# A two-layer graph network on one core: index buffers doubled from two to four, with the loops of GpSimd and SyncE unrolled over two bodies

## The reference, cut to what matters

```python
h   = node_features @ W_l1 * node_attr          # per node: 64 scalars and 32 vectors of 3
w   = silu(edge_scalars @ W_fc1) @ W_fc2        # per edge: 192 or 224 weights
hs  = h[edge_src]                               # gather, 160 floats for each edge
msg = products of w, hs and edge_attr           # per edge
agg = segment_sum(msg, edge_dst)                # scatter to the destination node
out = layernorm(x + self_term + agg @ W_out ...)
```

## Time and profile before

| | us |
|---|---|
| median of 3 runs | 7637.68 (7616.32 to 7642.06) |
| the profiled execution, its own time | 7651.23 |
| its span, first to last instruction | 7649.5 |
| PE matmul busy | 4892.6 (64%) |
| PE weight load busy | 3438.5 (45%) |
| POOL busy | 3010.1 (39%) |
| ACT busy | 2927.0 (38%) |
| DVE busy | 2467.3 (32%) |
| mean granted TensorE clock | 0.732 |

### The profile page before, as it was taken

How to read it: one execution, slowest core, us unless ns; L and a number is a source line. 1 busy time by engine, 2 the same in 40 slices (tenths; PEclk the granted TensorE clock), 3 DMA queues, 4 the chain that set the end, 5 groups by cost and what they waited for, 6 DMA issues and landing times. The chain is left out here.

```text
span 7649.5 us, 230407 instructions
## 1 busy us (share of the span) xinstructions
PE 4892.6 (64%) x91130; PEld 3438.5 (45%) x91131; DVE 2467.3 (32%) x6461; ACT 2927.0 (38%) x12105; POOL 3010.1 (39%) x3206
## 2 busy tenths in 40 slices
PE   6666666666666666666756666666666666666666
PEld 4444444444444444444644444444444444444445
DVE  3322222222222222222433333333333333333335
ACT  3333333333333333333434443444434444444445
POOL 4443434334334443344343333333333333343432
PEclk7777777777777777777877777777767777677777
DMA  3111111111111111111222221222211111111112
GB/s 96 45 45 43 45 44 45 44 43 47 40 38 39 39 39 39 38 39 39 79 55 55 56 57 54 56 55 54 56 53 51 50 49 49 49 51 50 51 49 75
DMA packets 361247, 381.97 MB, mean 50 GB/s; under 512 B 173041, under 2 KB 282421, under 8 KB 361086
## 3 DMA queue, kind: packets, MB, share of 16 engines
q0 software_dynamic: 150528, 257.10, 12.6%
q1 hardware_dynamic: 209360, 122.12, 6.0%
q10 hardware_dynamic: 1296, 1.91, 0.1%
HBM read 357.08 MB, written 23.76 MB: 50 GB/s over the span
## 5 line engine op out<-in xcount | busy, mean ns | idle before, releaser
L531 POOL DMA_INDIRECT e_rows<-scratch_table,k_index x3136 | 2963.1, 945 | 4476.9 <-DMA k_index<-in_src 2819.1
L590 PE MATMUL e_sum<-e_match,e_msg 128*32 128x40 f32 (+1 forms) x81536 | 2567.2, 236 | 2646.0 <-issue 2630.9
L590 PEld LDWEIGHTS e_sum<-e_match,e_msg 128*32 128x32 f32 x81536 | 1874.6, 125 | 3487.1 <-issue 3469.4
L554 ACT ACTIVATE e_match<-e_match,e_attr 128x40 f32<-128x40 f32 x10976 | 2482.7, 315 | 149.1 <-DMA e_attr<-in_edge_attr 118.9
L547 ACT ACTIVATE e_hidden<-e_h 100x512 f32<-100x512 f32 (+1 forms) x784 | 382.8, 488 | 4474.1 <-PE e_h L570 3772.4
L719 DVE TENSOR_TENSOR sums<-sums,e_sum 128x160 f32 x784 | 250.3, 319 | 3586.5 <-PE e_sum L590 1902.3
L583 PE MATMUL e_w<-k_fc,e_hidden 100*128 100x192 f32 (+1 forms) x6272 | 1286.5, 433 | 6.6 <-issue 5.3
L583 PEld LDWEIGHTS e_w<-k_fc,e_hidden 100*128 100x128 f32 (+1 forms) x6272 | 1026.0, 233 | 527.9 <-issue 495.4
L570 PE MATMUL e_h<-e_inputs,k_fc 128*100 128x512 f32 (+1 forms) x1568 | 948.7, 696 | 70.3 <-issue 34.6
L783 DVE TENSOR_TENSOR e_msg<-e_w,e_rows 128x512 f32<-128x512 f32 x784 | 542.2, 692 | 1370.8 <-PE e_w L583 909.7
L788 DVE TENSOR_TENSOR e_msg<-e_w,e_rows 128x384 f32<-128x384 f32 x784 | 429.7, 548 | 0.0
(11 more groups left out here) (130 smaller groups left out, 1059.6 us busy)
## 6 DMA issues: line engine op xcount, KB each, us to landing
e_rows<-scratch_table,k_index POOLq DMA_INDIRECT x3136
e_inputs<-in_inputs SPq DMA_DIRECT2D x196, 256.0 KB
e_attr<-in_edge_attr SPq DMA_DIRECT2D x392, 24.0 KB
e_inputs<-in_inputs SPq DMA_DIRECT2D x196, 40.0 KB
e_xb<-in_xT SPq DMA_DIRECT2D x50, 128.0 KB
scratch_yT<-m_yT SPq DMA_DIRECT2D x10, 640.0 KB, 4.3
e_xb<-scratch_yT SPq DMA_DIRECT2D x50, 128.0 KB
k_index<-in_src SPq DMA_DIRECT2D x392, 4.0 KB, 5.7
```

Source lines behind the costliest of these rows:

```text
L531: pool.indirect_dma_start(out=rows[j][:, t, :], out_offset=None, in_=table_dram, in_offset=bass.IndirectOffsetOnAxis(ap=index[q][:, c:c + ...
L554: last = nc.scalar.activation(match[j][:, t, c, :], match[j][:, t, 4, :], ACT.Copy, scale=attr[q][:, e0 + t, e:e + 1])
L590: return nc.tensor.matmul(out[32 * g:32 * g + 32, c0:c0 + n, :], m[:, f:f + 32], m5[:, which:which + n, :], start=first and opens, stop=en ...
```

## The change

There are four index buffers in place of two. Buffer k belongs to a half body of an even (k = 0, 1) or an odd body (k = 2, 3). In the place where SP loaded the indices of half body 2i+q, it now loads those of half body 2i+q+2, one whole body later, into the buffer whose gathers have just landed. The waits before that load are the same. POOL waits on the semaphore of its own buffer; each buffer is filled once in two bodies, by a semaphore step of 32. To name the buffers in the code, the loops of POOL and SP now cover two bodies in each turn. The other engines' code is unchanged. The setup phase and the node phase load four buffers in place of two, and `src` is padded by two half bodies.

```diff
-    w["index"] = [... (f"k_index{q}", [P, 2 * TPG], I32) for q in range(2)]
+    w["index"] = [... (f"k_index{k}", [P, STEP], I32) for k in range(INDEX_BUFFERS)]
...
-            for q in range(2):
-                sp.dma_start(w["index"][q][:, :], d["src"][:, 2 * TPG * q:2 * TPG * (q + 1)]).then_inc(index_in, 16)
+            for k in range(INDEX_BUFFERS):
+                sp.dma_start(w["index"][k][:, :], d["src"][:, STEP * k:STEP * (k + 1)]).then_inc(index_in, 16)
...
         @block.sync
         def _(sp):
-            def load(i, q):
-                tiles = bass.ds((2 * i + q) * (2 * TPG), 2 * TPG)
-                if not isinstance(i, int):
+            def load(i, q, k):
+                later = not (isinstance(i, int) and i == 0)
+                if later:
                     for j in (2 * q, 2 * q + 1):
                         sp.wait_ge(gathered[j], GATHERED * i)
-                    sp.dma_start(index[q][:, :], d["src"][:, tiles]).then_inc(index_in[q], 16)
+                    sp.dma_start(index[k][:, :], d["src"][:, bass.ds((2 * i + q + 2) * STEP, STEP)]).then_inc(index_in[k], 32)
                     sp.wait_ge(hid_done, GPB * i - GPB + 2 * q + 2)
...
+            def body(i, parity, with_base):
+                for q in range(2):
+                    load(i, q, (2 * parity + q + 2) % INDEX_BUFFERS)
+                if with_base:
+                    load_base(i)
+                if with_base and L == 1 and not (isinstance(i, int) and i == 0):
+                    store_self(i - 1)
+            for parity in range(2):
+                body(parity, parity, True)
+            with sp.Fori(1, NT // 2) as pair:
+                for parity in range(2):
+                    body(2 * pair + parity, parity, True)
             if L == 1:
                 store_self(NT - 1)
-            with sp.Fori(NT, BODIES) as i:
-                load(i, 0)
-                load(i, 1)
+            with sp.Fori(NT // 2, BODIES // 2) as pair:
+                for parity in range(2):
+                    body(2 * pair + parity, parity, False)
+            for k in range(2):
+                sp.wait_ge(index_in[k], 16 * BODIES)
...
         @block.gpsimd
         def _(pool):
-            def gather(count, j):
-                q = j // 2
+            def gather(count, used, parity, j):
+                k = 2 * parity + j // 2
                 if not isinstance(count, int):
                     pool.wait_ge(prepared, 1)
-                    pool.wait_ge(index_in[q], count)
-                    pool.wait_ge(msg_done[j], count)
+                    pool.wait_ge(index_in[k], count)
+                    pool.wait_ge(msg_done[j], used)
+                elif parity:
+                    pool.wait_ge(msg_done[j], 16)
                 for t in range(TPG):
...
-            for j in range(GPB):
-                gather(0, j)
-            with pool.Fori(16, 16 * BODIES, 16) as count:
+            for parity in range(2):
                 for j in range(GPB):
-                    gather(count, j)
+                    gather(0, 0, parity, j)
+            with pool.Fori(32, 16 * BODIES, 32) as count:
+                odd = count + 16
+                pool.compute_val(odd)
+                for parity in range(2):
+                    for j in range(GPB):
+                        gather(count, odd if parity else count, parity, j)
```

More of the change, by code:

```diff
@@ L49 @@
 AHEAD = 2
+STEP = 2 * TPG
+INDEX_BUFFERS = 4
+assert BODIES % 2 == 0 and NT % 2 == 0 and INDEX_BUFFERS == 4
 GATHERED = 16 * TPG
@@ L83, in kept_tensors @@
         w[name] = ctx.enter_context(nc.sbuf_tensor("k_" + name, shape, dt))
-    w["index"] = [ctx.enter_context(nc.sbuf_tensor(f"k_index{q}", [P, 2 * TPG], I32)) for q in range(2)]
+    w["index"] = [ctx.enter_context(nc.sbuf_tensor(f"k_index{k}", [P, STEP], I32)) for k in range(INDEX_BUFFERS)]
     return w
@@ L207, in _ @@
             sp.wait_ge(tab_in, 16)
-            sp.wait_ge(index_in, 32)
+            sp.wait_ge(index_in, 16 * INDEX_BUFFERS)
         @block.gpsimd
@@ L459, in edge_phase @@
         prepared, zeroed = sem("prepared"), sem("zeroed")
-        index_in = [sem(f"index_in{q}") for q in range(2)]
+        index_in = [sem(f"index_in{k}") for k in range(INDEX_BUFFERS)]
         attr_in = [sem(f"attr_in{q}") for q in range(2)]
@@ L475, in _ @@
         def _(sp):
-            def load(i, q):
-                tiles = bass.ds((2 * i + q) * (2 * TPG), 2 * TPG)
-                if not isinstance(i, int):
+            def load(i, q, k):
+                later = not (isinstance(i, int) and i == 0)
+                if later:
                     for j in (2 * q, 2 * q + 1):
                         sp.wait_ge(gathered[j], GATHERED * i)
-                    sp.dma_start(index[q][:, :], d["src"][:, tiles]).then_inc(index_in[q], 16)
+                    sp.dma_start(index[k][:, :], d["src"][:, bass.ds((2 * i + q + 2) * STEP, STEP)]).then_inc(index_in[k], 32)
                     sp.wait_ge(hid_done, GPB * i - GPB + 2 * q + 2)
                 cols = 2 * layer.group_cols
-                if L == 0 and isinstance(i, int):
+                if L == 0 and not later:
                     sp.wait_ge(zeroed, 2)
                 sp.dma_start(inputs[q][0:layer.kin, :], d[f"inputs{L}"][:, bass.ds((2 * i + q) * cols, cols)]).then_inc(inputs_in[q], 16)
-                if not isinstance(i, int):
+                if later:
                     sp.wait_ge(sum_done, GPB * i - GPB + 2 * q + 2)
-                sp.dma_start(attr[q][:, :, :], d["edge_attr"][:, tiles, :]).then_inc(attr_in[q], 16)
+                sp.dma_start(attr[q][:, :, :], d["edge_attr"][:, bass.ds((2 * i + q) * STEP, STEP), :]).then_inc(attr_in[q], 16)
             def load_base(i):
-                if not isinstance(i, int):
+                if not (isinstance(i, int) and i == 0):
                     sp.wait_ge(sum_done, GPB * i - GPB + 2)
@@ L532, in gather @@
                         out=rows[j][:, t, :], out_offset=None, in_=table_dram,
-                        in_offset=bass.IndirectOffsetOnAxis(ap=index[q][:, c:c + 1], axis=0),
+                        in_offset=bass.IndirectOffsetOnAxis(ap=index[k][:, c:c + 1], axis=0),
                     ).then_inc(gathered[j], 16)
-            for j in range(GPB):
-                gather(0, j)
-            with pool.Fori(16, 16 * BODIES, 16) as count:
+            for parity in range(2):
                 for j in range(GPB):
-                    gather(count, j)
+                    gather(0, 0, parity, j)
[5 more added lines that the diff above has]
+                        gather(count, odd if parity else count, parity, j)
         @block.scalar
@@ L1136 @@
     ("attr", (P, NT, 3), F32),
-    ("src", (P, T), I32), ("dst_tile", (P, T), I32), ("dst_by_group", (GP, GQ, GE), I32),
+    ("src", (P, T + 2 * STEP), I32), ("dst_tile", (P, T), I32), ("dst_by_group", (GP, GQ, GE), I32),
     ("edge_attr", (P, T, 6), F32), ("inputs0", (NB0, EPAD), F32), ("inputs1", (2 * NB1, EPAD // 2), F32),
@@ L1198, in lay_out @@
     r["attr"] = by_partition(padded(np.concatenate([a["node_vec1"], a["node_vec1_n2"], a["node_vec1_n3"]], 1), NPAD))
-    r["src"] = by_partition(padded(a["src"], EPAD))
+    r["src"] = by_partition(padded(a["src"], EPAD + 2 * STEP * P))
     dst = padded(a["dst"], EPAD, NODES)
```

8 lines of the change are left out of this document (removed).

## The result

The changed kernel takes **7732.79 us** (median of 4 runs, 7729.44 to 7739.46) against 7638.03 us before: the ratio is 1.0131, with a 95% interval of 1.0111 to 1.0151. It is slower by 95 us, past the upper end of the predicted range, where a small gain was forecast. One of the nine executions of the kernel before that were timed beside e11 and e12 took 14962 us, where the other eight took about 7628; it is left out of their ratios.

The account below looks back on a forecast made before the run. It took PE to be the bound, its sums nearly stopped while POOL gathers. Layer 0's -29 us and layer 1's about 0 summed to -30 us, from the 7638 us median to 7610 us; range 7505 to 7725.

Parts of the forecast that it names:

- PE bounds, the index wait bounds nothing: Whole kernel: PE bounds, with 2630.9 us idle marked "issue"; POOL's 2819.1 us index wait bounds nothing directly.
- The sums stand still while POOL gathers, and a window is fixed work of 11.5 us: Both layers: PE's sums nearly stop during eight gathers; first gather to PE at speed is 11.51 us, whenever it starts.
- What is late next is msg_done: POOL's gathers: with indices already there, they next wait for DVE to be through with the rows; no separate size.
- The eight gathers stay together, evenly spaced: Gathers of a half body: they run in one piece, windows about evenly spaced at 18.6 and 19.0 us.
- The walk in layer 1 gives 19.0 us: One half body of layer 1, step by step: 19.0 us against 19.02, so about 0, ends -53 to +114 us.
- The release: From a group's last message product to POOL's first gather: taken as 0.30 us.
- the low clock: PE's granted clock at 0.50 after each window: 3.4 to 5.0 us; layer 1's walk leaned to 3.4.
- The walk in layer 0 gives 18.6 us: One half body of layer 0, step by step: 18.6 us against 18.75, bounds 18.0 and 18.95.
- the 29 us: Layer 0's forecast gain: -0.15 us for each of 196 half bodies, -29 us.
- The new loops, loads and their neighbours cost nothing: Moved and added work: attribute and input loads beside the gathers nothing, extra setup and node-phase index loads 0.
- The slower rival: Both layers: clock returns later, 4.5 to 5.0 us after each window; 7680 to 7790, near 7700 us; chance 0.33.
- No change, as the stutters are not the gathers' doing: Rival for PE's sums: their gaps belong to the code, so gather placement does not matter; 7638 us; chance 0.13.

Follow-up runs that it names:

- e11: Changed kernel, but each group's four gathers start on the same group's sum in the body before, four windows a body; 6419.0 us, 0.8418 of the kernel before.
- e12: Changed kernel, but a window of eight gathers starts only when the next group's edge weights are done; 7654.5 us, 1.0037 of the kernel before.
- e6: Changed kernel with only the start of the gathers put back to the old place, after SP's index load there; 7594.9 us, 0.9966 of the kernel before.
- e7: Changed kernel, but each window of eight gathers starts on the sum of group 0 or 2 of the body before; 7558.4 us, 0.9889 of the kernel before.
- e9: Changed kernel with 2 of each group's 4 gathers left out after the first bodies, so computing with old rows; 4484.0 us against 7644.7 before, one run.
- e8: Changed kernel with a body's sixteen gathers as one window, after the messages of its last group; 7677.4 us, 1.0048 of the kernel before.
- e10: Changed kernel with the old, later start of the gathers in layer 1 alone; 7633.5 us, 0.9985 of the kernel before.
- e3: Changed kernel with POOL waiting for a body's last messages before its first gather; 5009.5 us, 1.2072 of the kernel before on a chip where that takes 4150.2.

## Why the prediction was wrong, point by point

- *PE bounds, the index wait bounds nothing.* Right. The wait of 2819 us went and the kernel got slower; e6 moved the start later and e7 earlier, and the time changed with each (7595 and 7558 against 7734).
- *The sums stand still while POOL gathers, and a window is fixed work of 11.5 us.* Right: in layer 1 after the change it is 11.40 us (5921.27 to 5932.67), and e9 shows the cause. It holds more widely than was claimed: whether gathers come in fours, eights or sixteens, each eight of them take 10.9 to 11.4 us from the first gather to PE at pace, in the mean of each layer of e6, e7, e8, e10, e11, e12 and of both kernels. The tail alone is no constant (0.95, 1.65 and 3.0 us).
- *What is late next is msg_done.* Right: POOL's new wait is for the last message product of a group.
- *The eight gathers stay together, evenly spaced.* They do mostly (18.8 and 19.5 us), but it is the second group of one half body with the first of the next: by the order of the gathers in the trace, after the first few bodies a window begins with group 1 or 3 and runs on into group 2 or 0. For the time this made no difference that I could find.
- *The walk in layer 1 gives 19.0 us.* **This is the step that failed**: 19.50. Its mechanism stood, two terms were mis-sized. The release took 0.79 us, not 0.30 (I had read it off the gap between two gathers that wait for nothing), so the window starts 3.5 us into the half body and nothing of hidden layer and weights is left beside it (0.2 us, the walk had 0.57). And the low clock: I took 3.4 us after each window from the single place of layer 1 that I had a row for; its mean after the change is 4.8. The walk with 3.4 us gave 18.75 (I took 19.0 between that and 19.6); the window ends 0.4 us later (5932.67 is 14.9 us after the free sum's start, not 14.5), 57 matmuls are left and not 65 (-0.15), and a low clock of 4.8 us, 1.4 more at half pace, adds 0.7: 19.7, against 19.5 measured. The 3.4 us were wrong for the kernel before as well, whose mean in layer 1 is 4.2 us a half body: the walk and the 19.02 that it was held against did not have the same clock in them. The error of the value taken is 0.5 us x 196 = 98 us, near the 87 us that the layer lost.
- *The walk in layer 0 gives 18.6 us.* 18.80 in the stretch that the 18.75 comes from, and 18.66 over the whole layer, where the kernel before has 18.67. The low clock is 4.3 us a half body, near the value taken, and 4.4 before, so the 29 us were the difference between a walk and a baseline read from part of the layer. From the layer's ends the change there is -2 us, not -29.
- *The new loops, loads and their neighbours cost nothing.* Right, by e6.
- *The slower rival* (near 7700, from a clock return later than 4.3 us on) came nearest: its range of 7680 to 7790 held the result, and in layer 1 the clock does return after 4.8 us. It was right in part only, since by the estimate above a third of the layer's loss is not the clock's, and the layer did not enjoy 3.4 us before. The chances leaned on one row: the next windows of the same trace would have shown 5.9 and 5.1 us.
- *No change, as the stutters are not the gathers' doing.* Out, by e9 and e11. The Trainium skill, "SBUF — State Buffer", section "Who interferes with whom", has PE never waiting on anyone; on three of the four chips of the experiments, PE's sums were held by DMAs that POOL issues, at some 20 to 30 matmuls in 10 us. By what path, no run here shows.

## What to carry to other kernels

Taking away a wait of an engine that is not the bound does not remove its work, it moves it; ask what it will run beside at its new place, and for a transfer that disturbs the bounding engine the place is all that counts. Here gathers cost next to nothing beside a few long matmuls and nearly all of their time beside many short ones. The buffers alone lost 1.3%; with a start that is chosen, four short windows that each begin at the end of a sum, the same buffers gain 15.8%. (The same start with the old two buffers was not run, so what share of the gain needs the buffers is open.) And before one value of a term that varies goes into a sum, read it at several places of the trace: one row of 3.4 us stood for 3 to 6. Measure such a thing on more than one chip, since on another the same kernel was bound elsewhere and an added wait on POOL (e3) cost a fifth; e11 was not run there.

## What the runs showed of the hardware that was not expected

- The same program takes 4150 us on one chip and 7627 to 7645 us on three others, with the same duration of a gather (946 ns) and no stutter on the first. What differs is not known, nor whether it stays with the chip.
- While eight gathers run, a sum of small matmuls makes some 15 to 37 of them in 9 to 11 us; the hidden-layer and weight matmuls beside the same gathers keep their 1.10 and 1.47 us. In windows of eight the hold begins 0.3 to some 3 us after the first gather: 0.3 us in e12's layer 1, where the window meets a sum that is well under way, and 2.4 us in layer 0 of the changed kernel, where PE makes long matmuls first.
- It ends 1.6 to 1.8 us after the last of eight gathers (at times 1.0), but 0.95 us after the last of four and 3.0 us after the last of sixteen, so that eight gathers take 10.9 to 11.4 us from first gather to PE at pace, however they are grouped.
- After such a hold the granted clock stays at 0.50 for 3 to 6.4 us with PE at work again, in both kernels.
- From the end of DVE's last product to the gather that waits for it POOL took 0.79 us (5920.48 to 5921.27), against 0.30 us between gathers that wait for nothing.
